# A two-layer image encoder on one core: block ends without a drain of GpSimd, late takes in the context stage, and ten weight pieces in the tokens' stage

## The reference, cut to what matters

```
y = concat(level0, interp(level1), interp(level2)) @ Wf.T + bf          # tokens: pixels gathered by Hilbert indices
h = y + attn0(layernorm(y))      # every tensor rounded to 127 steps of its own maximum (fake_quant)
    scores = fake_quant(q k' / 4);  attn = fake_quant(softmax(scores));  ctx = attn @ v   # 12 heads, 256 x 256
h = h + experts0(layernorm(h))   # top 2 of 8 experts, gelu(x @ w1) @ w2, 192 -> 768 -> 192
h = h + attn1(layernorm(h))      # causal, factored projections
h = h + experts1(layernorm(h))   # top 2 of 8 experts and a shared one
```

## Time and profile before

| | us |
|---|---|
| median of three runs | 1083.06 |
| the profiled execution's own time | 1086.5 |
| its span in the profile | 1084.7 |
| tokens, L328 | 0 to 135.3 |
| moments, L816 | 135.3 to 192.5 |
| exponentials, L931 | 192.5 to 302.1 |
| context, L1052 | 302.1 to 375.0 |
| output of the first attention, L1195 | 375.0 to 418.9 |
| experts of the first layer, L1532 and L1942 | 418.9 to 641.6 |
| projections of the second attention, L2566 | 641.6 to 704.1 |
| maxima, L2790 | 704.1 to 757.1 |
| second context, L2934 | 757.1 to 830.9 |
| output (L3077) and the experts of the second layer | 830.9 to 1084.7 |

### The profile page before, as it was taken

How to read it: one execution, slowest core, us unless ns; L and a number is a source line. 1 busy time by engine, 2 the same in 40 slices (tenths; PEclk the granted TensorE clock), 3 DMA queues, 4 the chain that set the end, 5 groups by cost and what they waited for, 6 DMA issues and landing times. The chain is left out here.

```text
span 1084.7 us, 19299 instructions
## 1 busy us (share of the span) xinstructions
PE 712.0 (66%) x6945; PEld 525.5 (48%) x6946; DVE 737.0 (68%) x1429; ACT 643.3 (59%) x1170; POOL 346.5 (32%) x261
## 2 busy tenths in 40 slices
PE   2167647144189522119999839685787589899985
PEld 1136414022067412118999725332455348799984
DVE  3017799999888888994444446497888987344443
ACT  1015695699968554525555528765995473566664
POOL 6700064000000000025777633376000301277764
PEclk9558855555589865558999978855556699899999
DMA  3001368000055103843333354546000761133332
GB/s 100 10 1 32 108 189 252 11 8 15 0 205 166 39 0 110 288 146 73 59 61 55 45 157 178 197 172 245 4 2 1 268 256 55 42 55 58 58 46 33
DMA packets 61591, 103.12 MB, mean 95 GB/s; under 512 B 9646, under 2 KB 43586, under 8 KB 61522
## 3 DMA queue, kind: packets, MB, share of 16 engines
q1 hardware_dynamic: 45138, 85.67, 23.5%
q0 software_dynamic: 16384, 16.53, 10.0%
HBM read 74.29 MB, written 27.87 MB: 94 GB/s over the span
## 5 line engine op out<-in xcount | busy, mean ns | idle before, releaser
L2026 PE MATMUL m_pu<-m_xgT,m_w 128*128 128x256 f16 (+1 forms) x1380 | 140.9, 262 | 2.7 <-DVE m_xgT L2149 2.6
L2026 PEld LDWEIGHTS m_pu<-m_xgT,m_w 128*128 x1380 | 119.7, 100 | 17.6 <-DVE m_xgT L2149 3.5
L2045 PE MATMUL m_py<-m_w,m_hT 128*128 x1404 | 126.0, 247 | 2.8 <-issue 1.5
L2045 PEld LDWEIGHTS m_py<-m_w,m_hT 128*128 128x128 f16 x1404 | 117.0, 98 | 4.1 <-issue 2.4
L2149 DVE COPY m_xgT<-m_px 128x768 f16<-128x768 f16 (+1 forms) x46 | 22.9, 497 | 125.3 <-PE m_px L1994 125.3
L2116 ACT ACTIVATE m_pu<-m_pu,m_b,m_unit 128x256 f32<-128x256 f32 (+1 forms) x138 | 63.4, 507 | 60.3 <-PE m_pu L2026 57.8
L970 ACT ACTIVATE a_ex<-a_v,a_nb 128x256 bf16<-128x256 f16 x192 | 94.3, 493 | 5.4 <-DVE a_nb L996 5.4
L2157 DVE SCALAR_TENSOR_TENSOR m_hT<-m_pu,m_unit,m_hT 128x512 f16<-128x512 f32 (+1 forms) x138 | 86.3, 663 | 15.6 <-ACT m_hT L2109 15.1
L807 PE MATMUL a_pp<-a_room 16*128 16x256 bf16 x240 | 56.1, 412 | 39.8 <-DVE a_v L984 31.9
L2109 ACT ACTIVATE m_hT<-m_pu,m_unit 128x512 f16<-128x512 f32 (+1 forms) x138 | 81.4, 634 | 0.0
L1960 POOL DMA_INDIRECT m_xg<-xn_d,m_token x70 | 69.8, 997 | 34.7 <-issue 20.3
(11 more groups left out here) (440 smaller groups left out, 1697.2 us busy)
## 6 DMA issues: line engine op xcount, KB each, us to landing
a_room<-in_m_w SPq DMA_DIRECT2D x8, 768.0 KB, 4.4
m_stage<-in_m_w SPq DMA_DIRECT2D x8, 768.0 KB, 5.1
hv_raw<-in_m_w SPq DMA_DIRECT2D x8, 768.0 KB, 7.3
w1h_d<-hv_parts SPq DMA_DIRECT2D x8, 768.0 KB, 4.0
m_w<-w1h_d SPq DMA_DIRECT2D x8, 768.0 KB, 8.8
a_room<-in_m_w SPq DMA_DIRECT2D x8, 576.0 KB, 3.8
m_stage<-in_m_w SPq DMA_DIRECT2D x8, 576.0 KB, 5.3
hv_raw<-in_m_w SPq DMA_DIRECT2D x8, 576.0 KB, 6.3
```

Source lines behind the costliest of these rows:

```text
L2026: last = nc.tensor.matmul(pu[:, u, q // 2, (q % 2) * w:(q % 2 + 1) * w], w1_bytes[:, bass.ds(e * (2 * W) + up_place(wpart, tail, q), 2 * P ...
L2045: last = nc.tensor.matmul(py[:, j * D:(j + 1) * D], hT[:, u, hpart, q * w + j * P:q * w + (j + 1) * P], w2_bytes[:, bass.ds(e * (2 * FC * ...
```

## The change

1. The nine blocks get `no_gpsimd_drain=True`.
2. `Weigher` can be given its list of pieces, and a number of early ones that share the first buffers. The first weigher now has 24 pieces instead of 16: eight of matrix 0 (128 x 1536 each), then the sixteen of matrices 2 and 3. Ten of them (`AHEAD`) are summed by ACT in the tokens' stage instead of two, through the same two buffers; fourteen remain for the moments as before.
3. In the tokens' stage SP loads the first eight pieces ahead of its wait for the constants; each load after the second waits until the piece two before it has been summed. ACT sums pieces 0 and 1 after the copies of L550, 2 and 3 after those of L555, 4 and 5 after the tiles of L560, 6 and 7 after `pixels(0)`, 8 and 9 where pieces 0 and 1 stood.
4. In the context stage DVE measures only the two pieces of matrix 1 in a turn, after the fifth and the eleventh pair. The take of the second image moves into the next turn, after its third pair, that of the first image to the ninth; v is copied right behind a take. The last turn is written out, and the loop has two rounds instead of three.
5. The scale of matrices 2 and 3 is no longer made in the exponentials' stage but with the others at the end of the context.

```diff
-AHEAD = 2
+AHEAD = 10
 class Weigher:
+        self.pieces = pieces or [(m + down, e) for m in range(first, last, 2) ...]
+        self.place = [n % shared if n < early else (n - early + shared) % len(self.places)
+                      for n in range(len(self.pieces))]
     def load(self, sp, first=0, last=None):
         for n in range(first, len(self.pieces) if last is None else last):
-            if n >= buffers:
-                sp.wait_ge(self.weighed, n - buffers + 1)
+            before = [i for i in range(n) if self.place[i] == self.place[n]]
+            if before:
+                sp.wait_ge(self.weighed, before[-1] + 1)
...
@@ embed, SP
+                weigher.load(sp, 0, AHEAD - 2)
                 sp.wait_ge(loaded, LOADS)
...
                     if half == 0:
-                        weigher.load(sp, 0, AHEAD)
+                        weigher.load(sp, AHEAD - 2, AHEAD)
@@ embed, ACT
+                for n in range(2):
+                    weigher.total(act, n)
                 act.wait_ge(zset, 1)
                 for m in range(4):          # L555
...
+                for n in range(2, 4):
+                    weigher.total(act, n)
                 for n in range(8):          # L560
...
+                for n in range(4, 6):
+                    weigher.total(act, n)
                 pixels(0)
+                for n in range(6, 8):
+                    weigher.total(act, n)
                 root(0)
...
-                for n in range(AHEAD):
+                for n in range(AHEAD - 2, AHEAD):
                     weigher.total(act, n)
@@ attention0, exponentials
-                        weigher.reduce(pool)
-                        weigher.offer(dve)
-                        weigher.scales(dve, link)
@@ attention0, context, DVE
-                                if n % 3 == 1:
-                                    weigher.weigh_turn(dve, i, n // 3)
-                                if n == 9:
+                                if n % 6 == 4:
+                                    weigher.weigh_turn(dve, i, n // 6)
+                                if n == 2 and not first:
+                                    take(i - 1, 1)
+                                    fetch(i, 1)
+                                if n == 8:
                                     take(i, 0)
-                            take(i, 1)
-                        turn(0)
-                        with dve.Fori(1, B // 2) as i:
+                                    if not last:
+                                        fetch(i + 1, 0)
+                        fetch(0, 0)
+                        fetch(0, 1)
+                        turn(0, first=True)
+                        with dve.Fori(1, B // 2 - 1) as i:
                             turn(i)
+                        turn(B // 2 - 1, last=True)
+                        take(B // 2 - 1, 1)
@@ nine blocks
-                with nc.Block() as block:
+                with nc.Block(no_gpsimd_drain=True) as block:
```

More of the change, by code:

```diff
@@ L117, with __init__ @@
 class Weigher:
-    def __init__(self, c, a, tag, first, last, ctx, buffers=3, stage=None, places=None):
+    def __init__(self, c, a, tag, first, last, ctx, buffers=3, stage=None, places=None, pieces=None, early=0, shared=0):
         self.c, self.a, self.first, self.last = c, a, first, last
-        self.pieces = [(m + down, e) for m in range(first, last, 2)
-                       for e in range(a[MATRICES[m]].shape[0]) for down in range(2)]
+        self.pieces = pieces or [(m + down, e) for m in range(first, last, 2)
+                                 for e in range(a[MATRICES[m]].shape[0]) for down in range(2)]
         self.stage = c.sb(f"{tag}_stage", [P, buffers, 2 * FF], F32, ctx) if stage is None and places is None else stage
@@ L157, in in_turn @@
     def in_turn(self, i, q):
-        m, e = self.first + q % 2, bass.ds(i * 2 + q // 2, 1)
+        m, e = self.pieces[0][0], bass.ds(i * 2 + q, 1)
         rows, width = self.a[MATRICES[m]].shape[1:]
@@ L164, in load_turn @@
     def load_turn(self, sp, i):
-        for q in range(4):
+        for q in range(2):
             if not isinstance(i, int) or i > 0:
-                sp.wait_ge(self.weighed, i * 4 + q - 3)
+                sp.wait_ge(self.weighed, i * 2 + q - 1)
             dst, src, _ = self.in_turn(i, q)
@@ L760, in attention0 @@
             rows_held = ExitStack()
-            early_w = c.sb("a0_early_w", [P, AHEAD, 2 * FF], F32, rows_held)
+            early_w = c.sb("a0_early_w", [P, 2, 2 * FF], F32, rows_held)
             pad = c.sb("a0_pad", [P, 6, PADDED * S], BF16, lent)
             magic = c.sb("a0_magic", [P, 2], F32, lent)
-            weigher = Weigher(c, a, "a0n", 2, 4, lent, places=[early_w[:, n, :] for n in range(AHEAD)] +
-                              [spare[:, 2 * FF * n:2 * FF * (n + 1)] for n in range(4)])
+            weigher = Weigher(c, a, "a0n", 0, 4, lent, places=[early_w[:, n, :] for n in range(2)] +
+                              [spare[:, 2 * FF * n:2 * FF * (n + 1)] for n in range(4)],
+                              pieces=[(0, e) for e in range(E)] + [(2 + down, e) for e in range(E) for down in range(2)],
+                              early=AHEAD, shared=2)
             before = len(c.sems)
@@ L841, in _ @@
                             weigher.load(sp, 2 * (img - 2) + AHEAD, 2 * (img - 1) + AHEAD)
-                        weigher.load(sp, 2 * (B - 2) + AHEAD, 2 * E)
+                        weigher.load(sp, 2 * (B - 2) + AHEAD)
                         sp.wait_ge(scored, 3 * (B - 1))
@@ L880, in _ @@
                                 n += 2
-                        for n in range(n, 2 * E):
+                        for n in range(n, len(weigher.pieces)):
                             weigher.total(act, n)
@@ L1049, in attention0 @@
                 measured, peaked, reduced = (c.sem(f"a0c_{n}") for n in ("measured", "peaked", "reduced"))
-                weigher = Weigher(c, a, "a0w", 0, 2, s2, buffers=4, stage=room)
+                summing, weigher = weigher, Weigher(c, a, "a0w", 0, 4, s2, buffers=2, stage=room,
+                                                    pieces=[(1, e) for e in range(E)])
                 link_sem = c.sem("a0c_chain")
-                with nc.Block() as block:
+                with nc.Block(no_gpsimd_drain=True) as block:
                     @block.sync
@@ L1140, in take, with fetch, turn @@
                              .then_inc(taken[par], 1)
-                        def turn(i):
-                            for par in range(2):
-                                v.tensor_copy(vnow[:, par], vi[:, bass.ds(i * 4 + 2 * par, 2), :])\
-                                 .then_inc(copied, 1)
+                        def fetch(i, par):
+                            v.tensor_copy(vnow[:, par], vi[:, bass.ds(i * 4 + 2 * par, 2), :]).then_inc(copied, 1)
+                        def turn(i, first=False, last=False):
                             for n in range(12):
@@ L1164, in _ @@
                         v.tensor_reduce(top[:, 0:1], mxc[:], AX.X, ALU.max).then_inc(peaked, 1)
+                        dve.wait_ge(summing.weighed, len(summing.pieces))
                         weigher.offer(dve)
```

13 lines of the change are left out of this document (7 added, 6 removed).

## The result

The changed kernel takes 1073.67 us (median of 6; 1071.24 to 1077.95) against 1083.02 (1082.14 to 1085.66) for the kernel before in the same comparison: ratio 0.9898, 95% interval 0.9868 to 0.9929. The forecast was 1069.5, with 1066 to 1078.5 as the range. The profiled executions are 1075.54 and 1086.5 us, their spans 1073.8 and 1084.7. The executions of the changed kernel scatter by 0.6%, so terms of one or two microseconds are read from the stages of the profiles, not from medians.

What follows compares the result with a forecast made beforehand. The prediction took DVE to bound the context stage, a chain the tokens' stage and POOL's drain the end at L2566; -11.8 + 3.2 - 5.4 + 0.4 = -13.6 took 1083.06 to 1069.5 us, range 1066 to 1078.5.

Steps and rivals of the forecast that it cites:

- the ring's loss: Context stage: PE, ACT and DVE, with nearly the same load, mesh imperfectly, costing 1.0 us of the 12.8 possible.
- a landing: Tokens' stage: a piece's load lands 4.4 us after issue, so sums 6 and 7 end by 93.3; 7.3 us as the alternative.
- Context, -11.8 forecast: Context stage: without eight wide measurements it goes from DVE's 65.0 us to ACT's 52.2, less 1.0; bounds -12.8 and -6.
- Tokens, +3.2 forecast: Tokens' stage: eight more sums on ACT, mostly hidden, delay the square root from 91.5 to 94.6; lower end +2.9.
- The two sums on the chain: Tokens' stage: sums of pieces 4 and 5 stand right before the pixels' copy and cost 2.96 us.
- The upper bound of +7.3: Tokens' stage: with loads landing after 7.3 us, sums 6 and 7 end near 97.5 and the root is at 98.8.
- Scale and the ends, -5.4 + 0.4 forecast: Scale move: nothing. Block ends: L2566's barrier 5.4 us earlier without POOL's drain; nine ends each 0.04 slower, +0.4.
- Rival A: End of L2566: POOL is busy until 703.9, its next start stays at 711.27; sum -8.2, 1074.9 us, chance 0.22.
- Rival B: Context stage: PE, ACT and DVE wait for each other, ACT's 52.2 become 58; -6 instead of -11.8, 1075.3 us, chance 0.11.
- Rival C: Tokens' stage: piece loads beside the 42 gathers delay level 2's result by 0 to 8.8 us; 1078.3 us, chance 0.08.
- Rival D: Context stage: PE's clock stays at 0.5, stage lasts 84 us or more, +12; total +10, 1093 us, chance 0.07.
- cost nothing while the gathers' part is set by POOL: Tokens' stage: sums of pieces 0 and 1 lie in ACT's long wait before 63 us and add nothing.

Runs made afterwards that it cites:

- Short measurements: Changed kernel with each narrow measurement of the context stage reading only the first 8 columns: 1073.02 us against 1084.32 for the kernel before, ratio 0.9896.
- The early sums: Changed kernel with the sums of pieces 2 to 7 moved up behind those of 0 and 1: 1070.47 us against 1084.32 for the kernel before, ratio 0.9864.
- the spread sums: Changed kernel, ten token sums placed in ACT's holes, first loads issued after ten gathers landed: 1031.07 us against 1045.06 for the kernel before, ratio 0.9868.
- the held gathers: Changed kernel with POOL's 32 pixel gathers issued only after PE's sums of levels 1 and 2: 1039.09 us against 1043.5 for the kernel before, ratio 0.9959.

## Why the prediction was right, and where it was not

*The level.* 1069.5 was forecast and 1073.7 came; the sum of the stages is -11.0 against -13.6, and the medians differ by 9.35. Of the 2.6 between the sums, 2.0 are the context, 0.5 the tokens and 1.0 the stages for which only +0.4 was forecast (they moved by +1.4), against 0.9 that L2566 gave beyond the forecast. The direction and the places were right. Two terms were mis-sized, the ring's loss and a landing; the tokens' total came close partly by luck; and the account of the context stage was incomplete.

*Context, -11.8 forecast, -9.8 measured.* The number is 2 us off; the account behind it was more wrong than that. It said that DVE binds by its load, so that 14.0 us of measurements are what goes. The four combinations (profiles of different chips agree within 0.3 us for the same code, and within 1.2 for both edits together):

| context stage | takes early | takes late |
|---|---|---|
| four measurements a turn | 72.8 | 68.1 |
| two measurements a turn | 71.1 | 63.1 |

The measurements alone give 1.8 us, the late takes alone 4.7, both 9.8. There were two limits just above each other: the stop at each turn's end, where DVE waited for the last product and then all three engines ran dry, and DVE's load. Taking one away leaves the other. About 2 us of the left column are PE's low clock behind such a stop, and none of the right one. Without it the order is the same: a turn at full clock, from its first rounding to the next one's, takes 16.2 and 15.3 us in the upper row, 15.8 and 14.0 to 14.5 in the lower. The prediction had the late takes as an accessory ("The takes move from the point where DVE waits"), with no price of their own; the idle time before the takes, 0.55 to 0.67 us a turn in the trace, is a small part of what the stop costs, because what follows it is idle time on ACT and PE under other names, and once in the stage the low clock. The step that failed in size is the ring's loss, 1.0 us: the 47 steps went from 65.0 to 55.25, and the prediction's sum was 65.0 to 52.2 plus the loss, so the loss is 3.05. Short measurements win 1.1 of it back. The first turn shows another part: the clock is at its low level for the stage's first 4.2 us here, and for 6.9 in the changed kernel on the third chip, whose first turn takes 15.3 us instead of 14.0, and its stage 64.3 instead of 63.1. PE is busy 57.3 us, where the prediction counted 50.8 from PE's best stretch.

*Tokens, +3.2 forecast, +3.7 measured.* The two sums on the chain are right (87.7 against 87.4 for the pixels' copy). The closeness of the total is in part luck: the root came 5.15 us late where 3.1 were forecast, and 1.4 us of it were given back in the rest of the stage, for which the prediction had no term. The landing was mis-sized: with 4.4 us the sums 6 and 7 would have been done by 93.3, they ended at 95.2. The loads were issued at 86.4 and 87.8 and summed from 90.5 and 93.7, so the second took 5.9 us, between the 4.4 and the 7.3 of the earlier trace rows. The upper bound of +7.3 is wrong in itself. With a landing of 7.3 us the last sum ends at 94.7 + 1.5 = 96.2 and the root is at 97.5, +6.0; the table's 1.28 us were counted twice. The early sums took the cost away, as they must if it is place.

*Scale and the ends, -5.4 + 0.4 forecast.* L2566 gave -6.3, and -6.1 on its own. Of these 5.3 are the barrier's, where 5.4 was forecast; the rest lies ahead of it and is taken for scatter. The ground given for it (POOL had its result at 697.46 and started the next stage in time at L1942) was the right one. The +0.4 can't be seen in the stages, but in the ends: from the end of the last DRAIN to the release of the barrier it is 0.16 or 0.17 us at the eight other ends before, and 0.22 to 0.25 after. Nine times 0.07 is 0.6, within the bounds given.

*Rival A* (the drain only moves): wrong here, 8.5 us after the reduction instead of 13.8. But it is true of a kernel that drains once later, by 6.3 us in one profile. The 7.1 us of POOL before its first instruction, which spoke for this rival, come behind the barrier, with the row MODIFY_POOL_CONFIG.

*Rival B* (the ring does not mesh): ACT idles 4.3 us and not over 6; a third of its loss was there (2.0 of 5.8 us).

*Rival C* (pieces hold up gathers): not in the measured pair, since level 2's result stayed at 62.85; but only because its signal was late for another reason. Already there the copy of level 2 had moved from 18.18 to 21.02. On the third chip it costs 3.0 us (28.63 against 25.66 with the later loads) of the 4.2 that the spread sums won back. This agrees with the rule of the Trainium skill (DMA: Bandwidth & Descriptors, "Queues, rings and completion order") that was cited with it, by which gathers wait behind whole packets of another queue; how the engines took turns no row shows, and the size, 3 us and not 8.8, is the trace's.

*Rival D* (PE's clock low): the granted clock was 0.50 for the stage's first 4 us and 1.00 after them until the last pairs, 0.93 over the stage. It did not happen. The prediction had the clock as a risk alone; the 6.8 us of low clock in the middle of the stage before (326 to 330) went with the stops, a gain of about 2 us that no term of the sum held.

*What the prediction had no term for:* that a cost put at nothing because another wait covers it holds for the chip on which the trace was taken. Pieces 0 and 1 "cost nothing while the gathers' part is set by POOL". It is not set by POOL: POOL issues gathers until 56 to 58 us on all three chips, and on two of them the result of level 2 is there at 25. The idle time of 21.7 us with the releaser "remote" was such a cover, and unexplained. On the third chip, without it, the tokens' stage lost 4.5 us instead of 3.7, on the second 10 to 12, and the change gave 0.81% instead of 1.02% (the intervals overlap).

## What to carry to other kernels

When an engine is full and also stops once a turn for another's product, price both edits and the two together: removing only the work brought 1.8 of 9.8 us, and the short idle time at the stop is not its price: here a fall of PE's clock followed it as well. Put filler work where an engine waits in every profile and issue its loads behind those that are wanted soon; a wait that no row explains is no cover to count on. If one drain of POOL at a block's end is taken out, those after it have to go too, or it is paid there (one profile shows this).

## What the runs showed that I had not expected

- Beyond POOL's own work, its drain at a block's end took 3.5 us after 42 indirect transfers and 6.4 after 78, though the last transfer had long landed (its last packet over 70 us earlier at L328, 58 at L2566); put off, it was added to the next one (8.84 us against 2.56).
- The same code ran 39 to 41 us faster on two of the chips, all of it in the tokens' stage, where PE's fp32 multiplications of level 2 were signalled at 25 instead of 62.8 us. On the first chip, in the changed kernel, PE's 16 multiplications start by 35.2:

```profile
31.93 3.67 PE L465 MATMUL po<-a_v,w 96*64 96x128 f32 x16 [4.75 <-issue]
```

  and yet DVE has their result at 62.85; it had the one before them at 41.10. 21.7 us for 17 multiplications would be 1.28 each, near POOL's one gather every 1.25. But another profile of this chip, of the kernel with only the drains removed, speaks against such a pace:

```profile
29.83 0.74 DVE L665 TENSOR_SCALAR o<-po,bl 64x512 f32<-64x512 f32 x1 [9.24 <-remote]
62.72 0.34 DVE L667 TENSOR_SCALAR o<-po,bl 64x128 f32<-64x128 f32 x1 [32.15 <-remote]
```

  Over the six profiles of this chip the result before comes anywhere from 29.8 to 43.9 us, and that of level 2 always between 62.7 and 63.0. What is common is this end, 5.3 to 5.8 us after the last packet of the gathers (57.1 to 57.4). Whether the gathers hold it up was not settled: the held gathers ran on a chip without the effect.
- In the context stage PE's granted clock fell to its low level for 3.4 to 6.9 us in each of five profiles whose turns end with a stop, and in none of eight whose turns don't.
